# Attention results turned in blocks of 32 by VectorE in place of TensorE's transposes, in a three-part transformer block on one Trainium2 core

## The reference

```python
x = x + 0.5 * ffn(layernorm(x))
x = x + attn(layernorm(x))
x = x + 0.5 * ffn(layernorm(x))

# attn: 16 heads of 16 dimensions
q, k = layernorm per head of x @ Wq.T and x @ Wk.T, times 256 ** -0.25
v = x @ Wv.T
att = softmax(q @ k.T, causal)
return (att @ v) @ Wo.T + bo
# ffn: base matrix + shared low-rank part + two of six routed low-rank parts (rank 16 each)
```

## Time and profile before

| | |
|---|---|
| Median of three runs | 1348.42 us |
| The profiled execution's own time | 1348.32 us |
| Its span in the trace | 1346.6 us |
| PE (matmul) busy | 1165.6 us, 87% |
| ACT busy | 1021.1 us, 76% |
| DVE busy | 454.8 us, 34% |
| POOL busy | 235.0 us, 17% |
| Mean granted TensorE clock | 0.954 of full speed |

### The profile page before, as it was taken

The page is one execution under the profiler, slowest core; times in us unless marked ns, Lnnn a source line. Parts: engine busy times, 40 slices in busy tenths (PEclk is TensorE's granted clock), DMA queues, the critical chain, the costliest instruction groups (busy, mean ns, idle before and its releaser), DMA issues.

```text
span 1346.6 us, 23146 instructions
## 1 busy us (share of the span) xinstructions
PE 1165.6 (87%) x9076; PEld 385.2 (29%) x9076; DVE 454.8 (34%) x1164; ACT 1021.1 (76%) x1132; POOL 235.0 (17%) x377
## 2 busy tenths in 40 slices
PE   2636778999899979999899999899999999999974
PEld 2522323333232323322223223222222222222223
DVE  4655534445244424343233232322222111011113
ACT  2213546778688868888888899798999999999960
POOL 2223422323112210121101102101102101010000
PEclk9767988999899989999999999999999999999986
DMA  4011200101200030000300002100001200000000
GB/s 130 1 53 35 72 1 24 57 1 36 77 1 1 25 88 1 1 1 25 87 1 2 1 0 72 40 1 1 1 1 39 58 0 2 8 9 1 9 9 16
DMA packets 39674, 33.39 MB, mean 25 GB/s; under 512 B 8787, under 2 KB 39497, under 8 KB 39561
## 3 DMA queue, kind: packets, MB, share of 16 engines
q1 hardware_dynamic: 37360, 31.74, 7.9%
q10 hardware_dynamic: 2200, 0.12, 0.1%
HBM read 18.73 MB, written 12.85 MB: 23 GB/s over the span
## 4 chain that ended last, share of the span: by engine, by line
PE 62%; ACT 14%; DVE 10%; issue 7%; SPq 2%; DMA 2%; POOL 1%; ACTq 1%; DVEq 0%; POOLq 0%
PE ps L1101 56%; ACT ring L708 14%; PE ps L1140 2%; PE ps L1201 1%; DVE xnT L780 1%; SPq L540 1%; PE ps L1309 1%; DMA x<-in_x 1%; DVE oT L1081 1%; DVE st L739 1%; DVE xnT L778 1%; PE ps L1317 1%; PE ps L1160 1%; DVE area L760 1%; DVE area L934 1%
## 5 line engine op out<-in xcount | busy, mean ns | idle before, releaser
L708 ACT ACTIVATE ring<-ps 128x1024 f32<-128x1024 f32 x1056 | 989.7, 1103 | 166.5 <-PE ps L1101 163.9
L1101 PE MATMUL ps<-ring,vf 128*17 128x512 f32 (+3 forms) x4608 | 564.8, 568 | 3.8 <-POOL ring L662 2.9
L1101 PE MATMUL ps<-queries,keys 50*128 50x512 f16 (+3 forms) x2304 | 379.2, 369 | 35.6 <-DMA queries<-shift_d 9.8
L1101 PEld LDWEIGHTS ps<-queries,keys 50*128 50x128 f16 x2304 | 93.5, 93 | 505.1 <-ACT ring L708 433.4
L662 POOL TENSOR_SCALAR_AFFINE_SELECT ring<-ring 128x256 f32<-128x256 f32 (+1 forms) x224 | 98.4, 457 | 462.9 <-ACT ring L708 461.5
L1101 PEld LDWEIGHTS ps<-ring,vf 128*17 128x17 f32 x4608 | 80.3, 96 | 174.5 <-issue 145.7
L778 DVE CAST xnT<-ps 128x512 f16<-128x512 f32 x50 | 34.5, 690 | 126.0 <-PE ps L1140 110.8
L649 POOL TENSOR_TENSOR rstd<-var,minus_half 128x4 f32<-128x4 f32 x24 | 24.4, 1016 | 268.6 <-DVE var L745 268.5
L1081 DVE COPY oT<-ps 128x512 f32<-128x512 f32 x32 | 22.1, 690 | 144.9 <-PE ps L1101 144.9
L1101 PE MATMUL ps<-baseT,xnT 128*128 128x256 f16 x384 | 56.7, 287 | 7.6 <-DVE area L780 1.8
L912 DVE SCALAR_TENSOR_TENSOR x<-ps,power,x 128x512 f32<-128x512 f32 x32 | 24.0, 750 | 113.9 <-PE ps L1101 113.9
(11 more groups left out here) (145 smaller groups left out, 704.0 us busy)
## 6 DMA issues: line engine op xcount, KB each, us to landing
parts_d<-split SPq DMA_DIRECT2D x32, 256.0 KB, 2.6
keys<-parts_d SPq DMA_DIRECT2D x96, 64.0 KB, 2.3
queries<-parts_d SPq DMA_DIRECT2D x192, 32.0 KB
x<-in_x SPq DMA_DIRECT2D x8, 512.0 KB, 4.0
out_x<-x SPq DMA_DIRECT2D x16, 256.0 KB, 2.2
queries<-shift_d SPq DMA_DIRECT2D x64, 4.0 KB
ring<-in_base_W SPq DMA_DIRECT2D x1, 256.0 KB, 3.9
ring<-in_Wq SPq DMA_DIRECT2D x1, 256.0 KB, 4.9
```

Of the source, the lines that this page charges most:

```text
L708: act.activation(probs[:, u % RING, :], bank(2 * (u % SLOTS), 2), ACTF.Exp, bias=0.0, scale=1.0).then_inc(exp_ok, 1)
L1101: return pe.matmul(o, lhsT, rhs, start=start, stop=stop, skip_group_check=True)
```

## The change

`gather` becomes a VectorE transpose of the bank ACC into `oT`, which turns each block of 32 partitions by 32 columns within itself. Partition 32k + t then holds, for head k, token t of each of the 16 blocks of tokens, with the 16 results and the sum side by side. `divide` has no PE share any more: VectorE takes 16 reciprocals per partition and multiplies, from SBUF to SBUF. `att` is laid out as two halves of 16 blocks of 32 columns; a block of 32 holds head k of two groups next to each other. `turnout` has no PE share either: VectorE transposes one half back (32 by 32), copies it as half precision and subtracts to get the low part, from SBUF. The semaphore `att_ok` counts the halves, and PE's `projout` waits for both of a chunk.

For the rows to come out in the order that Wo wants, the heads are computed in another order (`HEAD`): the transposed Wq and Wk are written with their groups of 16 columns exchanged, once at the start, and `values` takes `vf[:, j, HEAD[h], :]`. In the last chunk, half 0 is turned right after the second group's `divide`, and the parts go to `xnT[1]`, with `sq` and `qT[1]` as scratch; in the other chunks to `xnT[2]`, with `area[2]` as scratch. `divide` and `turnout` no longer use bank 7.

```diff
+HEAD = [h // 8 * 8 + h % 4 * 2 + h % 8 // 4 for h in range(NH)]
 def output(c):
-    for stage in ("turnout", "projout"):
-        for a in range(2):
-            yield 1.5, stage, (c, a)
+    if c < NC - 1:
+        yield 1.5, "turnout", (c, 0)
+    for stage, a in (("turnout", 1), ("projout", 0), ("projout", 1)):
+        yield 1.5, stage, (c, a)
...
         if groups and groups[0][0] <= u:
-            yield "divide", groups.pop(0)[1]
+            k = groups.pop(0)[1]
+            yield "divide", k
+            if k == NG * (NC - 1) + 1:
+                yield "turnout", (NC - 1, 0)
...
                     dve.wait_ge(pv, LAST_BATCH[n] + 1)
-                    dve.tensor_copy(oT[:, :], bank(ACC)).then_inc(acc_read, 1)
+                    if n >= 1:
+                        dve.wait_ge(*main.own.at())
+
+                    dve.transpose(oT[:, :], bank(ACC)).then_inc(acc_read, 1)
                 elif stage == "divide":
                     g = n % NG
-                    tiles = bank(main.bank["divide", n]).rearrange("p (n q c) -> p n q c", n=TC, q=GH)
-                    dve.wait_ge(main.ready, main.use["divide", n])
-                    dve.reciprocal(den[:, :, :], tiles[:, :, :, HS]).then_inc(*main.own.up())
+                    turned = oT[:, :].rearrange("p (q c) -> p q c", c=32)
+                    dve.wait_ge(acc_read, n + 1)
+                    dve.reciprocal(den[:, :], turned[:, :, HS]).then_inc(*main.own.up())
                     dve.wait_ge(*main.own.at())
-                    dve.tensor_tensor(att[:, :, g * GH * HS:(g + 1) * GH * HS].rearrange("p n (q c) -> p n q c", q=GH), tiles[:, :, :, 0:HS],
-                                      den[:, :, :].unsqueeze(3).broadcast_to([P, TC, GH, HS]), ALU.mult).then_inc(main.read, 1)
+                    dve.tensor_tensor(att[:, g // 2, :, g % 2 * HS:(g % 2 + 1) * HS], turned[:, :, 0:HS],
+                                      den[:, :].unsqueeze(2).broadcast_to([P, CH // 32, HS]), ALU.mult).then_inc(*main.own.up())
+                elif stage == "turnout":
+
+                    c, i = n
+                    back_ = (sq, qT[1])[i][:, :] if c == NC - 1 else area[2][:, i * CH:(i + 1) * CH]
+                    parts = att_parts(c)
+                    dve.wait_ge(*main.own.at())
+                    dve.transpose(back_, att[:, i, :, :].rearrange("p q c -> p (q c)")).then_inc(*main.own.up())
+                    dve.wait_ge(*main.own.at())
+                    dve.tensor_copy(parts[:, 0, i, :], back_).then_inc(*main.own.up())
+                    dve.wait_ge(*main.own.at())
+                    dve.tensor_tensor(parts[:, 1, i, :], back_, parts[:, 0, i, :], ALU.subtract).then_inc(att_ok, 1)
...
+                    if k in (3, 4):
+                        o, turner = o.rearrange("p (g h d) -> p g h d", g=2, d=HS), turner.rearrange("p (h g d) -> p g h d", g=2, d=HS)
+                    m = mm(o, src, turner, i == 0, i == len(blocks) - 1)
...
-                    m = mm(bank(ACC)[32 * k:32 * k + VL, q0:q0 + w], vf[:, j, h, :], probs[...], first, last)
+                    m = mm(bank(ACC)[32 * k:32 * k + VL, q0:q0 + w], vf[:, j, HEAD[h], :], probs[...], first, last)
...
-                elif stage == "divide":
-                    b = side_bank(main, ("divide", n))
-                    pe.wait_ge(acc_read, n + 1)
-                    for i in range(TC):
-                        m = pe.transpose(b[:, i * P:(i + 1) * P], oT[:, i * P:(i + 1) * P], ident[:, :])
-                    m.then_inc(main.ready, 1)
-                elif stage == "turnout":
-                    c, a = n
-                    b = side_bank(main, (stage, n))
-                    pe.wait_ge(*main.done["divide", NG * c + NG - 1])
-                    for ib in range(2):
-                        for i in range(2):
-                            m = pe.transpose(b[:, ib * D + i * P:ib * D + (i + 1) * P], att[:, 2 * a + i, ib * P:(ib + 1) * P], ident[:, :])
-                    m.then_inc(main.ready, 1)
                 elif stage == "projout":
                     c, a = n
                     b = side_bank(main, (stage, n))
-                    pe.wait_ge(*main.done["turnout", n])
+                    pe.wait_ge(att_ok, 2 * (c + 1))
```

More of the change, by code:

```diff
@@ L254 @@
 BANK_STAGES = ("sizes", "turn0", "turn1", "turn2", "inner0", "inner1", "turnin0", "turnin1", "outer0", "outer1", "qk", "value", "heads",
-               "divide", "turnout", "projout")
-SPLIT_STAGES = ("turn0", "turn1", "turn2", "turnin0", "turnin1", "turnout")
+               "projout")
+SPLIT_STAGES = ("turn0", "turn1", "turn2", "turnin0", "turnin1")
 def on_scalar(stage, n):
@@ L286, with __init__ @@
 class Pass:
-    def __init__(self, name, semaphore, order, banks, scalar, x, x_in):
+    def __init__(self, name, semaphore, order, banks, scalar, x, x_in, fronts):
         def s(q):
@@ L300, in __init__ @@
         self.high_act = s("high_act")
[L301 to L304, removed]
+        self.xn_ok, self.var_ok, self.rstd_ok = ([s(f"{q}{i}") for i in range(fronts + 1)] for q in ("xn_ok", "var_ok", "rstd_ok"))
+        self.lg_ok, self.ex_ok = ([s(f"{q}{i}") for i in range(fronts)] for q in ("lg_ok", "ex_ok"))
+        self.wt_ok = [s(f"wt_ok{i}") for i in range(fronts)]
+        self.hw_ok = [s(f"hw_ok{i}") for i in range(fronts)]
         self.sq_ok, self.ss_ok, self.norm_ok, self.high_ok, self.low_ok = (s(q) for q in ("sq_ok", "ss_ok", "norm_ok", "high_ok", "low_ok"))
@@ L373, in build @@
         oT = sb("oT", [P, CH])
-        att = sb("att", [P, TC, D])
+        att = sb("att", [P, 2, CH // 32, 32])
         ones = oT[0:2, 0:CH // 2].bitcast(F16)
-        zeros = att[0:2 * NH, :, :].rearrange("p n d -> p (n d)").bitcast(F16)
+        zeros = att[0:2 * NH, :, :, :].rearrange("p i q c -> p (i q c)").bitcast(F16)
         ident = sb("ident", [P, P])
@@ L420, in build @@
         tmp = sb("tmp", [P, TC, 2 * NH])
-        den = sb("den", [P, TC, GH])
+        den = sb("den", [P, CH // 32])
         ps = ctx.enter_context(nc.psum_tensor("ps", [P, 8 * CH], F32))
@@ L437, in build, with att_parts @@
             "gen_in", "gen_mm", "gen_max", "gen_tr", "gen_copy", "gen_out"))
-        s_ok, exp_ok, mask_ok, pv, acc_read, bo_ok = (semaphore(q) for q in ("s_ok", "exp_ok", "mask_ok", "pv", "acc_read", "bo_ok"))
+        s_ok, exp_ok, mask_ok, pv, acc_read, bo_ok, att_ok = (semaphore(q) for q in (
+            "s_ok", "exp_ok", "mask_ok", "pv", "acc_read", "bo_ok", "att_ok"))
+        def att_parts(c):
+            return xnT[1 if c == NC - 1 else 2]
         def x_main(c):
             return x_all[:, c % XS, :, :]
-        main = Pass("m", semaphore, ORDER, START_BANKS, on_scalar, x_main, lambda c: (x_in[c], 16))
+        main = Pass("m", semaphore, ORDER, START_BANKS, on_scalar, x_main, lambda c: (x_in[c], 16), 2)
         gen = Pass("g", semaphore, [q for c in range(NC) for q in general_order(c)], (SIDE,), lambda *_: False, lambda c: xg,
-                   lambda c: (gen_in, 16 * (c + 1)))
+                   lambda c: (gen_in, 16 * (c + 1)), 1)
         out_v = out[0].rearrange("(n p) d -> p n d", p=P)
@@ L499, in moved @@
         def moved(stage, n, b, part=0):
-            if stage in ("turn0", "turn1", "turn2", "turnout"):
+            if stage in ("turn0", "turn1", "turn2"):
                 c, a = n
-                i = {"turn0": 0, "turn1": 1, "turn2": 2, "turnout": 2}[stage]
+                i = int(stage[-1])
                 return xnT[i][:, part, :, a * D:(a + 1) * D], bank(b).rearrange("p (b t) -> p b t", b=2)
@@ L635, in _ @@
             pool.memset(oT[0:2, 0:CH // 2].bitcast(F16), SHIFT).then_inc(const, 1)
-            pool.memset(att[:, :, :], 0.0).then_inc(const, 1)
+            pool.memset(att[:, :, :, :], 0.0).then_inc(const, 1)
             pool.memset(vf[:, :, :, HS:HS + 1], 1.0).then_inc(const, 1)
@@ L1129, in weight @@
                 for i, (src, rows, cols, at) in enumerate(blocks):
-                    m = mm(bank(k % 3)[0:cols, at:at + rows], src, turners[0:rows, k, 0:rows], i == 0, i == len(blocks) - 1)
+                    o, turner = bank(k % 3)[0:cols, at:at + rows], turners[0:rows, k, 0:rows]
+                    if k in (3, 4):
+                        o, turner = o.rearrange("p (g h d) -> p g h d", g=2, d=HS), turner.rearrange("p (h g d) -> p g h d", g=2, d=HS)
+                    m = mm(o, src, turner, i == 0, i == len(blocks) - 1)
                 m.then_inc(K.w_turned, 1)
@@ L1292, in values @@
                 for q0, k, h, j, w, u, bk, col in blocks:
-                    m = mm(bank(ACC)[32 * k:32 * k + VL, q0:q0 + w], vf[:, j, h, :], probs[:, u % RING, bk * CH + col:bk * CH + col + w], first, last)
+                    m = mm(bank(ACC)[32 * k:32 * k + VL, q0:q0 + w], vf[:, j, HEAD[h], :], probs[:, u % RING, bk * CH + col:bk * CH + col + w], first, last)
                 m.then_inc(pv, 1)
```

2 lines of the change are left out of this document (1 added, 1 removed).

## The result

The changed kernel takes 1329.82 us (median of 4 runs, 1325.4 to 1331.56). Beside it the kernel before took 1350.03 (1347.44 to 1353.62). The ratio is 0.9843, 95% interval 0.9808 to 0.9879, so 20.2 us are saved, where the forecast of 1321 stood for 27.

What follows compares the result with a forecast made beforehand. PE's queue was taken to bound chunks 0 to 6, ACT chunk 7, an engine-to-engine chain the tail. Savings of 20 + 4 + 0 + 3.6 = 27.6 us from 1348.3 gave 1321 us; own range 1309 to 1333, wider range 1302 to 1342.

Steps and rivals of the forecast that it cites:

- The group ends: At the 31 divides before the last, PE's queue gets shorter and bank 7 is freed: 20 us saved, ends 10 and 36.
- The queue's 1.14 us per place: PE's queue at each divide: 0.58 us waiting for the copy of ACC plus 0.56 for transposes, counted at 16 places.
- Starts of chunks: Turnout and projout at chunk starts: projout 1.3 us earlier in chunks 1, 2 and 7, 4 us saved; chunks 3 to 6, 0.
- I write 0 for the four together: Starts of chunks 3 to 6, behind the input's DMA: no net gain; ends 4 us saved and 5 lost.
- The clock's 1.26 us: Projout after the stall at starts of chunks 3 to 6: 12 matmuls at PE's lower clock, 2.74 us against 1.48.
- Behind the last unit: In the tail, from the copy to projout, 7.12 us become 3.5: 3.6 us saved, 1.3 more if PE's clock stays high.
- The price of the transposes: A 32 by 32 transpose of 128x512 f32 on DVE costs 0.69 us, as the copy from the same bank does.
- Only the idle directly behind counts: Rival, chance 0.14: divides bring 10 us rather than 20, starts of chunks nothing, the tail 3.6; total 1335 us.
- Two passes: Rival, chance 0.13: each DVE transpose takes 1.22 us, so 14.9 us less gain; total 1336 us.
- the slow transpose: Rival, chance 0.06: DVE's transpose from PSUM takes 2.28 us and frees ACC late; 1380 us, about 1395 at worst.
- More than the sum: Rival, chance 0.09: with fewer bank 7 steps every side step moves up; divides bring 36 us, chunk 0 another 8; 1297 us.
- ACT's waits for PE: Sign that the forecast is right: ACT's waits for PE over the whole span fall from 163.9 to about 140 us.

Runs made afterwards that it cites:

- the idle transposes: Changed kernel with four unread transposes of the identity put back on PE at each divide, bank 7 not held for the division: 1337.08 us, ratio 0.9921.
- the second profile: The changed kernel measured and profiled once more without an edit: 1328.14 us, ratio 0.9853.
- The experiment on both kernels: Next chunk's side work begun 10 units later from chunk 3 on: 1301.38 us on the changed kernel, 1332.85 us on the kernel before.
- the kernel whose tail was edited: Changed kernel with half 0 of the last chunk turned only behind the last unit, right ahead of half 1: 1322.93 us, ratio 0.981.

## Why the prediction was right, and where a size was off

*The group ends* (20 forecast, 21.8 measured). The step held. The queue's 1.14 us per place is near what the idle transposes take back (on average 1.0 at each of 12 places, where I had 16). With the fifth taken off, the sum had 14.6 for the queue, 4 for bank 7 and 1.6 for chunk 0; measured are about 13, 7 and 1.9. The bank was worth more than I gave it and the queue a little less, so the sum is closer than its parts: that much is luck. What comes last instead at the group end of the earlier trace rows is the masks, as the changed kernel's row at 284.89 shows (0.59 us); their wait rose from 5.6 to 25.4 us in all, though most of that is at the starts of chunks.

*Starts of chunks* (-4 forecast, +4.2 measured). This is the term that was mis-sized, by 8 us, most of the 9 by which the profiled span missed. Three sentences of it failed, each differently.

"Projout begins at 1074.4: 1.3 us earlier. The same in chunks 1 and 2": chunk 7 did so, 1.9 earlier, with projout 0.29 behind the subtraction:

```profile
1059.36 1.47 PE L1127 MATMUL ps<-woT,xnT 128*128 128x256 f16 x12 [0.29 <-DVE xnT L1115]
```

Chunks 1 and 2 didn't: the subtraction takes 2.72 in chunk 1 and 1.15 in chunk 2, in both profiles of this kernel. In chunk 2 projout also ran at the lower clock, 2.62 us behind 1.82 of waiting; that was chance, for in the second profile it took 1.47 behind the same 1.82. In chunk 1 it was at the lower clock before the change too (2.74). I had priced the subtraction from the earlier trace rows, where one input comes from PSUM; now both lie in SBUF. The Trainium skill has this, in "SBUF — State Buffer", section "SBUF: two separate sides": a DVE instruction with two SBUF inputs and a GpSimd one lock each other out for a whole instruction. The trace agrees: POOL's addition ends at 169.21 + 2.51 = 171.72, DVE's subtraction at 172.27. No row shown before the change had it; I should have cited it as a rival to the price.

"... this wait stays and moves on PE from turnout to projout": in chunk 5 it did (4.69 us for L1115). In chunks 3 and 4 PE stops earlier, at values behind POOL's masks (7.80 and 8.14), since the masks queue behind `rstd`. Before, PE stood at the turnout's transposes in that time (7.12 in chunk 4), so the masks' delay hardly showed.

"I write 0 for the four together; the ends are 4 saved and 5 lost": +4.2, at the bad end, and 6.6 in the second profile, beyond it. The clock's 1.26 us came as priced in chunks 4, 5 and 6 (2.72 against 1.47); the 1 us I set against it did not, since in chunks 5 and 6 the transposes had run at 0.63 before, with nothing to save. In chunk 5 two waits that were apart became one of 4.69, and ACT then idles 6.69. The experiment on both kernels says what the step missed in kind: the DMA's wait doesn't just add zero there, it absorbs 6 to 15 us of what the change gives (26 to 35 less 20; 12 by place). Without it, chunks 3 to 6 win the same 1.9 us each as chunk 7.

*Behind the last unit* (-3.6 forecast, -1.7 measured). Up to projout it is right to the digit: 7.12 us became 3.55. The clock stayed low at projout (2.71), so the extra 1.3 did not come. The loss is at the very end: the last outer matmuls ran at the lower clock in this profile, 1.46 us for what took 0.83 in the profile before. The first row is the changed kernel's, the second the kernel before's.

```profile
1321.17 1.46 PE L1127 MATMUL ps<-baseT,xnT 128*128 128x256 f16 x6 [0.85 <-DVE x L924]
```

```profile
1341.02 0.83 PE L1101 MATMUL ps<-baseT,xnT 128*128 128x256 f16 x6 [0.85 <-DVE x L912]
```

That is chance in the kernel before, not a cost of the change. In the profile of the kernel before with its side steps late, which leaves the tail as it is, the clock stayed low to the end, and the tail was 47.4 us, not 45.8. Low against low, 47.4 became 44.1: 3.3 us, near the 3.6 of the forecast. Leaving aside the kernel whose tail was edited, the tails of the changed kernels lie between 41.2 and 44.3. Why the clock rises there in some executions stays open.

*The price of the transposes* (0.69 forecast, 0.72 and 0.70 measured). By the rule cited in the prediction it costs what a copy does, and the trace agrees.

*The rivals.* "Only the idle directly behind counts" (1335) is out: the group ends brought 21.8, not 10. "Two passes" didn't happen; made to happen in `gather` at 0.75 each, it cost about 5 us, where my 20 places would have made 15. For the same reason the slow transpose was priced too high: even at 0.75 more per group end the kernel stays 15 us ahead of the one before, and since 0.75 costs only 5 us there, the point where the change would lose lies beyond the 1.3 us I gave (argued, not run; the transposes of the turnouts were not doubled). "More than the sum" gave bank 7 too much, but named the right hindrance: with the DMA out of the way the change is worth 26 to 35.

*ACT's waits for PE* fell to 153.1, not 140. ACT's idle time as a whole fell from 213.6 us to 1185.21 - 985.83 = 199.4: where a chunk starts behind the DMA, a wait returned what the group ends had saved.

## What to carry to other kernels

Price work taken off an engine as queue time plus the buffer that it held, place by place, and count only places where the bound engine then waits: that forecast 20 us at the group ends, and 21.8 came. Then look for the one in-order queue with a foreign wait in it (here DVE behind an input DMA): it absorbs gains made elsewhere. Moving that stage by 10 units gave 17 us alone, the change 20 alone, and the two together 46. Ask also which queue makes the wait long: here half of it had passed before SP issued the load. And where an operand moves from PSUM to SBUF, price the instruction anew, with its neighbours on POOL.

## What the hardware did that I had not expected

A 128x512 subtraction with both inputs in SBUF took 2.72 us beside a POOL addition of 2.51, and 0.69 alone. A cast from SBUF took 0.43 us alone, 0.68 and 0.77 at two places beside POOL's masks, and 0.43 at a third. A 32 by 32 transpose of 128x512 f32 costs DVE the same from PSUM (0.72) and from SBUF (0.70). And a wait can have an aftermath: behind 3.6 us of idle PE's next 12 matmuls took 2.71 us, behind 0.3 us 1.47. In between, the wait's length doesn't settle it: behind the same 1.82 us they took 2.62 in one profile and 1.47 in the other.
